# Both token norms turned by DMAs, feed-forward maxima one step later, ScalarE applying the second norm

## The reference, cut to what matters

```
x = x + _L0_conv_ref(_gn(x), ...)                      # gate, two experts of four, ReLU between w1 and w2
t = _to_tokens(x)                                      # (32, 784, 96)
t = t + _L1_attn_ref(_ln_t(t), qkv_w, ..., proj_b)     # 12 heads of 8, A = sum over tokens of fk * fv, out = q A
t = t + _L1_ffn_ref(_ln_t(t), W1, b1, W2, b2)
# _ln_t:  (v - mean) / sqrt(var + 1e-5) over the 96 channels of a token
# _L1_ffn_ref: y = x @ sign(W1).T + b1; y is scaled by 128 / max|y| of its group and clipped; gelu;
#              the same with W2.  There are 5 groups of 6 images; images 30 and 31 give zero.
x = _from_tokens(t, x)
```

## Time and profile before

| | us |
|---|---|
| median of 3 runs (lowest to highest) | 776.96 (775.61 to 778.39) |
| the profiled execution's own time | 777.66 |
| its span in the trace | 776.0 |
| PE busy | 727.5 (94%) |
| DVE busy | 679.7 (88%) |
| ACT busy | 473.3 (61%) |
| POOL busy | 221.5 (29%) |

### The profile page before, as it was taken

How to read it: one execution, slowest core, us unless ns; L and a number is a source line. 1 busy time by engine, 2 the same in 40 slices (tenths; PEclk the granted TensorE clock), 3 DMA queues, 4 the chain that set the end, 5 groups by cost and what they waited for, 6 DMA issues and landing times.

```text
span 776.0 us, 15540 instructions
## 1 busy us (share of the span) xinstructions
PE 727.5 (94%) x4858; PEld 480.5 (62%) x4858; DVE 679.7 (88%) x2058; ACT 473.3 (61%) x669; POOL 221.5 (29%) x301
## 2 busy tenths in 40 slices
PE   6798899999999999999999999999999899999991
PEld 3465466666766666766666766666766566555550
DVE  3577589999999999999999999999999678999997
ACT  2455356665555665555665555665554699999980
POOL 2352223324333324333324333324332001111110
PEclk8889899999999999999999999999999999999996
DMA  9970111111111111111111111111110101564446
GB/s 216 199 186 1 32 33 32 34 47 31 31 47 31 31 47 31 31 47 31 31 47 31 31 47 31 31 47 31 31 31 16 31 1 19 91 127 60 62 63 140
DMA packets 17663, 41.40 MB, mean 53 GB/s; under 512 B 4553, under 2 KB 4839, under 8 KB 17639
## 3 DMA queue, kind: packets, MB, share of 16 engines
q1 hardware_dynamic: 14552, 33.27, 16.4%
q0 software_dynamic: 2688, 7.23, 6.6%
q10 hardware_dynamic: 399, 0.60, 0.3%
HBM read 22.28 MB, written 18.67 MB: 53 GB/s over the span
## 4 chain that ended last, share of the span: by engine, by line
PE 63%; DVE 18%; issue 6%; ACT 5%; SPq 3%; DMA 2%; POOL 2%; DVEq 1%; ACTq 0%; POOLq 0%
PE slot L1071 15%; PE slot L1055 13%; PE slot L1284 6%; PE slot L1077 5%; PE slot L917 5%; PE slot L1082 5%; PE slot L1131 5%; DVE stage L1659 4%; PE slot L1118 4%; ACT stage L799 4%; SPq L476 3%; DVE stage L1646 3%; DVE y2max L1765 2%; DVE xn L1788 1%; PE slot L1342 1%
## 5 line engine op out<-in xcount | busy, mean ns | idle before, releaser
L1071 PE MATMUL slot<-hT,w2s 128*96 128x392 f32 x372 | 132.6, 492 | 0.8 <-DVE w2s L1532 0.8
L1613 DVE TENSOR_SCALAR tok<-tok,ln_mv,ln_rs 112x96 f32<-112x96 f32 x434 | 109.0, 322 | 2.0 <-POOL ln_rs L624 1.9
L624 POOL TENSOR_TENSOR ln_rs<-ln_ve,pow_half 112x7 f32<-112x7 f32 (+2 forms) x92 | 105.1, 1142 | 7.2
L799 ACT ACTIVATE stage<-slot,kv_bias,kv_unit 112x768 f32<-112x768 f32 (+1 forms) x62 | 53.1, 907 | 86.6 <-PE slot L1118 86.6
L621 POOL TENSOR_TENSOR ln_ve<-ln_mv,ln_eps 112x7 f32<-112x7 f32 (+2 forms) x92 | 18.3, 199 | 296.1 <-DVE ln_mv L1595 296.1
L792 ACT ACTIVATE hT<-slot,b1c,w_unit 128x784 f32<-128x784 f32 x93 | 93.1, 1004 | 15.8 <-PE slot L1055 13.2
L1082 PE MATMUL slot<-big,W1b 96*128 (+1 forms) x360 | 89.3, 329 | 0.0
L1071 PEld LDWEIGHTS slot<-hT,w2s 128*96 128x96 f32 x372 | 58.6, 163 | 45.0 <-issue 42.9
L1619 DVE TENSOR_REDUCE ymax<-slot 128x784 f32 (+1 forms) x90 | 84.5, 966 | 0.0
L1077 PE MATMUL slot<-big,W1b 99*128 (+1 forms) x360 | 84.4, 329 | 0.0
L854 ACT ACTIVATE hT<-slot,s 128x784 f32<-128x784 f32 x90 | 80.2, 914 | 6.1 <-DVE stage L1646 3.2
(11 more groups left out here) (252 smaller groups left out, 1455.4 us busy)
## 6 DMA issues: line engine op xcount, KB each, us to landing
xs<-in_x SPq DMA_DIRECT2D x32, 294.0 KB, 2.9
out<-h_second SPq DMA_DIRECT2D x32, 294.0 KB, 2.6
big<-in_x SPq DMA_DIRECT2D x7, 1176.0 KB, 15.5
out<-h_second POOLq DMA_DIRECT2D x24, 294.0 KB, 4.2
big<-out SPq DMA_DIRECT2D x1, 1764.0 KB, 10.5
out<-big SPq DMA_DIRECT2D x6, 294.0 KB, 2.7
big<-in_x SPq DMA_DIRECT2D x2, 588.0 KB, 24.5
con<-shape_consts ACTq DMA_DIRECT2D x1, 445.5 KB, 6.3
```

What stands on the lines that cost most here:

```text
L624: nc.gpsimd.tensor_tensor(ln_rs[n][:, j0:j1], ln_ve[n][:, j0:j1], pow_half[0:TOK, j0:j1], ALU.pow).then_inc(ln_rstd[part], 1)
L799: nc.scalar.activation(ekv[:, j0:j0 + n, :], chunks(k, n, 256, 2 * C), ACT.Exp, bias=kv_bias[:, :], scale=kv_unit[0:TOK, 0:1]).then_inc(e_ ...
L1071: ins = mm(S[k][0:C, h, 0:HALF], w2s[:, v, t, :], src[:, t, h * HALF:(h + 1) * HALF], start=t == 0, stop=t == last, skip_group_check=True)
L1613: ins = V.tensor_scalar(src[:, j, :], src[:, j, :], ln_mv[n][:, j, 0:1], ln_rs[n][:, j:j + 1], ALU.subtract, ALU.mult)
```

## The change

Neither norm's tokens are transposed on PE any more. ACT makes a float16 high part of the tokens as they stand (112 tokens on the partitions, seven chunks padded from 96 to 128 columns), DVE the low part, and SP turns each part with one transposing DMA, from SBUF to SBUF: x1 into `xh1_hi` and `xh1_lo`, x2 straight into `big`. The padding carries the rows of ones (one for the attention's bias, three for the feed-forward bias), which is what L668 and a memset did before. The pads are written by POOL once, after the setup tensors whose memory they reuse.

The second norm is applied by ACT as scale and shift (seven activations, `apply2`), for which POOL forms -mean and its product with 1/sqrt; its moments are taken in one part. The maxima of the feed-forward tiles are taken for image i-3 instead of i-2: the first tile stands on PE behind mix and ahead of keys and values, in slot 2, and waits for both parts of x2; the second (tile 2, slot 0) stands behind A, the third (tile 1, slot 2) behind St's product. The hidden tiles run in the order 1, 0, 2, and mix in the same; t2's transposes stand between the first and the second mix. Image 29's three tiles come after the loop, ahead of the last keys and values, and the filling matmuls there are gone. On POOL, `xn_rest` goes first in a step and waits no longer for the norms. On SP, a step has four transposing DMAs beside the load and the store, in a written order.

```diff
+            def move_x1(i):
+                sp.wait_ge(x1_hi_ready, i)
+                if isinstance(i, int) and i == 1:
+                    sp.wait_ge(pads_ready, 1)
+                else:
+                    sp.wait_ge(ao_ready, i - 1)
+                sp.dma_start_transpose(turned(xh1_hi[:, 0:HW]),
+                                       x1_hi[:, :, :].rearrange("p j c -> p (j c)")).then_inc(x1_hi_moved, 16)
+                sp.wait_ge(x1_lo_ready, i)
+                sp.dma_start_transpose(turned(xh1_lo[:, 0:HW]),
+                                       x1_lo[:, :, :].rearrange("p j c -> p (j c)")).then_inc(x1_lo_moved, 16)
...
+            for i in range(LAST):
+                if i >= 1:
+                    move_x1(i)
+                if i >= 3:
+                    move_x2_low(i - 3)
+                if i >= 2:
+                    store_last((i - 1) // 2, (i - 1) % 2)
+                if i < LAST - 2:
+                    load_next(i // 2, i % 2)
+                if i >= 2:
+                    move_x2_high(i - 2)
+            move_x2_low(QIMAGES - 1)
+            store_last(LAST // 2 - 1, 1)
+            move_x1(LAST)
             store_last(LAST // 2, 0)
...
+            def x1_high(i):
+                act.wait_ge(xh1_ready, i)
+                nc.scalar.copy(x1_hi[:, :, 0:C], tok1[:, :, :]).then_inc(x1_hi_ready, 1)
+            def apply2(f):
+                act.wait_ge(ln_shift, f + 1)
+                for j in range(CHUNKS):
+                    ins = nc.scalar.activation(tok2[:, j, :], tok2[:, j, :], ACT.Identity,
+                                               scale=ln_rs[1][:, j:j + 1], bias=ln_nm[:, j:j + 1])
+                ins.then_inc(xh2_ready, 1)
...
@@ TensorE, one step
+                    pe.wait_ge(h_ready, 3 * i + 1)
+                    mix(1, 1, 1, first=1)
+                    if norm2:
+                        pe.wait_ge(t2_ready, i - 1)
+                        to_tokens(3, t2T[r], tok2_in_psum)
+                    pe.wait_ge(h_ready, 3 * i + 2)
+                    mix(1, 1, 0, first=1)
+                    pe.wait_ge(h_ready, 3 * i + 3)
+                    mix(1, 1, 2, first=1).then_inc(y_mixed, 1)
+                if ffn:
+                    pe.wait_ge(x2_hi_moved, 16 * (i - 2))
+                    pe.wait_ge(x2_lo_moved, 16 * (i - 2))
+                    ffn_next(0)
                 if attend:
-                    pe.wait_ge(xh1_hi_ready, i)
+                    pe.wait_ge(x1_hi_moved, 16 * i)
...
@@ VectorE, one step
+                if attend:
+                    x1_low(i)
...
                 if ffn:
-                    dve.wait_ge(tok2_ready, f + 1)
-                    stats2(f)
+                    x2_low(f)
+                if norm2:
+                    dve.wait_ge(tok2_ready, i - 1)
+                    stats(1, tok2, i - 1)
...
+                if ffn:
+                    absmax(f, 0)
...
                 if ffn:
-                    for t in range(SPLIT):
-                        absmax(f, t, t)
+                    absmax(f, 1)
+                    absmax(f, 2)
...
+                if experts:
+                    apply1(i)
```

More of the change, by code:

```diff
@@ L616, in _ @@
             nc.gpsimd.tensor_scalar(kv_bias[:, :], kv_bias[:, :], -1.0, 1.0, ALU.add, ALU.mult).then_inc(kvw_ready, 1)
[L618 to L625, removed]
+            pool.wait_ge(kvw_ready, 2)
@@ L632, in step @@
[L632 to L636 removed]
+                    shift(i - 2)
                 rstd(0, i)
@@ L835, in step @@
                     nc.scalar.copy(R_hi[:, :], S[3][0:C + 1, 0, 0:C]).then_inc(r_hi_ready, 1)
-                if experts and next_:
+                if next_:
                     norm_image(m + 1, r, i + 2)
-            step(0, 0, attend=False, ffn=False, between=True)
+                if norm2:
+                    x2_high(i - 2)
+            step(0, 0, attend=False, norm2=False, high=False, between=True)
             for i in range(1, FIRST):
-                step(i // 2, i % 2, ffn=i >= 2)
+                step(i // 2, i % 2, norm2=i >= 2)
                 if i == 2:
@@ L847, in _ @@
             step(LAST // 2 - 1, 0, next_=False)
-            step(LAST // 2 - 1, 1, next_=False)
+            step(LAST // 2 - 1, 1, next_=False, high=False)
             def gelu_tile(g, b, t, k=None):
@@ L1219, in step @@
                     mix(1, 1, 0, h_second)
-                elif experts and not first:
-                    pe.wait_ge(h_ready, 3 * i + 2)
-                    mix(1, 1, 0)
-                if attend and not second:
-                    x1_to_channels()
-                if second:
                     mix(1, 1, 2, h_second)
@@ L1589, in chunk_stats, with stats @@
                 return ins
-            def moments(part, count):
-                n, j0, j1 = LN_PARTS[part]
-                wait_apart(dve, ln_stats[part], count, dve_passed)
-                for j in range(j0, j1):
+            def stats(n, src, count):
+                chunk_stats(src, range(CHUNKS)).then_inc(ln_stats[n], 1)
+                wait_apart(dve, ln_stats[n], count, dve_passed)
+                for j in range(CHUNKS):
                     ins = V.bn_aggr(ln_mv[n][:, j, :], ln_st[:, j, :])
-                ins.then_inc(ln_mean[part], 1)
@@ L1617, in absmax, with apply1, x1_low @@
-            def absmax(f, t, k):
-                dve.wait_ge(y_ready, 3 * f + t + 1)
+                ins.then_inc(ln_mean[n], 1)
+            def apply1(i):
+                dve.wait_ge(ln_rstd[0], i + 1)
+                for j in range(CHUNKS):
+                    ins = V.tensor_scalar(tok1[:, j, :], tok1[:, j, :], ln_mv[0][:, j, 0:1], ln_rs[0][:, j:j + 1],
+                                          ALU.subtract, ALU.mult)
+                ins.then_inc(xh1_ready, 1)
+            def x1_low(i):
+                dve.wait_ge(x1_hi_ready, i)
+                V.tensor_tensor(x1_lo[:, :, 0:C], tok1[:, :, :], x1_hi[:, :, 0:C],
+                                ALU.subtract).then_inc(x1_lo_ready, 1)
@@ L1734, in step @@
                                            ALU.mult, ALU.add).then_inc(t2_ready, 1)
-                if ffn and not last:
-                    absmax(f, SPLIT, SPLIT)
-                if experts and not last:
-                    apply(0, tok1, i).then_inc(xh1_ready, 1)
             for i in range(FIRST):
-                step(i // 2, i % 2, attend=i >= 1, ffn=i >= 2)
+                step(i // 2, i % 2, attend=i >= 1, norm2=i >= 2, ffn=i >= 3)
                 if i == 1:
```

340 lines of the change are left out of this document (165 added, 175 removed).

## The result

| | before | after |
|---|---|---|
| median, us (lowest to highest) | 777.56 (775.61 to 778.39), 4 runs | 855.65 (849.41 to 859.06), 4 runs |
| profiled execution, time / span | 777.7 / 776.0 | 853.6 / 851.9 |

The changed kernel is slower: the ratio is 1.100, 95% interval 1.093 to 1.107. The direction was forecast; the size was not: 802 was predicted, and 856 lies outside the range of 763 to 850.

A forecast was written before the change was run, and what follows sets the result against it. TensorE, issuing in order almost without a hole, was taken to bound the kernel, VectorE nearly as full. 777.7 us + 23 (29 steps at 17.45) + 2 (ends) = 802.7, or 802 as a median; range 763 to 850.

The forecast's parts named there:

- ACT's activations: Seven second-norm activations on ACT: 1.7 us a step, up to 2.3, hidden below PE's step; St's lateness beyond set to nothing.
- PE's saving: PE's step without the normed tokens' transposes: 16.15 us if no transfer is late, at most 0.5 us saved.
- DVE's times and the queue's start: Subtractions on DVE 0.80 us each, x2_low made by T+5.5; SP issues x1 high at T+3.9.
- T: Start of the step's first hidden matmul on PE, from which the forecast counts times in us.
- Landing: Transfer of x2's low part: 3.2 us from issue to landing, so there at T+8.9.
- L: Issue-to-landing time of a transposing DMA: bounds 2.0 to 4.2 us, taken as 3.2.
- Issue time: SP's time to issue each transposing DMA in its queue, taken as 0.9 us.
- r: Issue time of one transposing DMA on SP: bounds 0.34 to 1.4 us, taken as 0.9.
- The rival of a bound by SP's issue: SP's queue: r of 1.4, x2 low at T+10.4, step 18.9 us, kernel 846 us; chance 0.20.
- The clock in the loop: Half clock behind a PE hole, a hidden pair 0.86 us for 0.5: only some 3 us at the ends, for the range.
- The ends: Outside the steady steps: step 2 takes 2.0 us less, the part behind the loop +4; net +2 us.
- a landing like the plain store's: No-change rival, x2 low's transfer: L 2.55 to 2.65 us, step 16.65, kernel 778 us; chance 0.08.

The follow-up runs named there:

- e11_older_split: e1_older with ScalarE rearranged: next norm moved ahead of its image's cast, second norm's activations split four before St, three behind R_hi; 766.06 us.
- e1_older: Changed kernel with feed-forward tiles reading token parts one image step older, all transfers still made; 782.50 us, ratio 1.0086.
- e6_low_split: Changed kernel with x2's low part made and sent at the end of the step before, and ScalarE rearranged as in e11_older_split; 770.53 us.
- e7_order_split: e5_order with the rearranged ScalarE of e6_low_split; 785.86 us, ratio 1.0108.
- e2_fill: Changed kernel with eight filling matmuls of 512 columns ahead of TensorE's wait for x2's parts; 840.15 us, ratio 1.0807.
- e8_four_chunks: Changed kernel with x1's two transfers turning only four of seven chunks from image 2 on; 845.30 us, ratio 1.0873.
- e10_one_chunk: Changed kernel with x1's two transfers turning only one of seven chunks from image 2 on; 839.53 us, one run.
- e5_order: Changed kernel with x2's low part ahead of x1's low part on VectorE and in SP's queue; 803.82 us, ratio 1.0322.
- e3_apply_late: Changed kernel with ScalarE's seven second-norm activations moved behind its copy of R_hi; 894.79 us, ratio 1.1518.

## Why the prediction was wrong, step by step

The runs split the 2.45 us by which a steady step grew (19.08 less 16.63). The rows add up by construction, since each is the difference of two runs:

| part | us a step | from |
|---|---|---|
| what the edit saves when nothing is late | -0.64 | e11_older_split 15.99, before 16.63 |
| ACT's activations, St late | +0.47 | e1_older 16.46 less 15.99 |
| wait for x2's low part | +2.04 | 18.50 less 16.46 |
| clock behind that wait | +0.58 | 19.08 less 18.50 |

What speaks for each row beyond the sum: ACT's other order gave 0.47, 0.45 and 0.47 on three different kernels (e11_older_split, e6_low_split, e7_order_split); the wait is 2.02 from start to start in the trace; and e2_fill takes the clock's part away while the wait stays. The first row includes ACT's other order, in which the next norm also stands elsewhere, so it is the saving of the edit in its best form and not of the edit as it was made.

- **PE's saving.** Forecast 16.15 at best, measured 15.99. Right, to 0.16.
- **DVE's times and the queue's start.** Forecast x1 high at T+3.9 and x2_low made by T+5.5; measured 406.42 - 402.56 = T+3.86, and 0.85 after 407.20, T+5.49. Right to a tenth, subtractions included (0.77 from start to start, for 0.80).
- **Landing.** L taken as 3.2, measured 3.09 in this place. Right.
- **Issue time: the first step that failed.** r was taken as 0.9, by the 138 KB SBUF-to-SBUF row; it is 1.21 to 1.29. Together with the gaps between issues, x2 low was issued at T+6.45, not T+5.7, and landed at T+9.54, not T+8.9; PE was ready for it at T+7.52, not T+7.66. The wait, in the forecast's own terms, is 2.0 instead of 1.3: +0.7. The upper bound of 1.4, by a small parameter load, would have been nearer. The rival of a bound by SP's issue gave 846, for r = 1.4; the queue is what holds x2 low back, as it says, though e8_four_chunks and e10_one_chunk refute its reason by the tile. On the Trainium skill, DMA: Bandwidth & Descriptors, Why a DMA increments its semaphore by 16 and not by 1: its count per tile led me to an estimate of four times the ordinary issue, which 1.21 beside 0.34, 3.6 times, nearly bears out, but the trace does not agree with the count itself, since 7 tiles cost 1.12. The factor of four was loose besides: 49 times 32 is 1568 cycles, three times the 512, and four only if the 512 come on top. Advanced Engine Details and Errata, X-Bar Transpose (TRN2), as fast as ordinary: the landing of 2.7 to 2.8 beside the store's 2.8 comes near, though for two thirds of its bytes; the issue does not agree.
- **The clock in the loop: the second.** I had the earlier trace rows, a 2.65 us hole with a pair at 0.86 behind it, and kept it for the ends only, 3 us in the range. The forecast itself put a hole of 1.3 us in each of 29 steps and priced them at full clock. With the 1.9 that came it costs 0.58 a step, 17 us. At e5_order's 0.54 it costs nothing; no run has a hole of 1.3, so whether the forecast's own hole would have been free stays open.
- **ACT's activations: the third.** 1.7 in all, up to 2.3, were forecast from a copy of 97 columns (0.24 each); they take 2.61 (373 ns from start to start; the 457 ns of the groups' row count each by itself, with the overlap). The text had named the point: over 2.3, St comes late, "a term that I set to nothing". It was 0.47: in e1_older the product with St starts 0.40 later than in e11_older_split, and what follows it another 0.07.
- **The ends.** +2 forecast (step 2 included); measured +2.7, the 75.9 less the 73.2 by which the 29 steps from image 3's first hidden tile (115.52 for 119.11 before) to the loop's last matmul grew. The sum is right, its parts are not, and that is luck. What follows the loop grew by 6.3 instead of 4, though keys and values begin 8.7 behind its last matmul, for 8.4 forecast. Step 2, forecast 2.0 shorter, took 18.5 for 18.0. And image 2 started 4.1 earlier, which the forecast did not have: image 0's transposes start at 77.12 for 81.46 already, and why is open (in the edits image 2 starts anywhere from 96.6 to 99.8). The idle time behind the loop was forecast as about 4 us and is 4.48, with six matmul pairs at half clock behind it.
- **Readings that were off and changed nothing.** The clock's slices in the earlier trace rows are at 9 from the sixth to the last but one, not from the fourth: the fifth is an 8. For a landing like the plain store's, 5.5 + 2.6 is T+8.1, which makes a step of 16.6 and not 16.65.

In the forecast's terms a step should have been 17.45 and was 19.08: -0.16 for the saving, +0.74 for the wait, +0.58 for the clock, +0.47 for ACT, together 1.63, 47 us over 29 steps. The profiled execution took 853.6, 51 more than the 802.7. The other 4 are the loop's first steps, which were longer than the steady ones (19.15 is the mean with them), the ends, and rounding.

## What to carry to other kernels

Take a transfer that replaces engine work by its place in the queue: count every issue ahead of it at its own price, and ask where its consumer stands; here the same four transposes hold PE up by 2 us a step or not at all, 70 us in all, by the position of one subtraction and one issue. Price each new hole of an otherwise full TensorE twice, once for itself and once for half clock that can follow it, from a hole of similar length in the trace, and as a chance: here about half of equal holes cost it. A mean busy share of 61% is no slack: look for the chain that the inserted work stands in (ACT from R_hi to the ReLUs), and pair a move into it with a move out of it.

## What the runs showed of the hardware

- A transposing DMA from SBUF to SBUF holds the issuing engine 1.21 us (high parts) to 1.29 (low parts) for 196 KB, and 1.12 to 1.23 for a seventh of it; an ordinary store behind it 0.57 instead of 0.34.
- From issue to landing such a transfer took 2.7 us (median, x1's high part, 196 KB), 2.3 with four chunks of seven and 2.2 with one; as the third in a row 3.09.
- The kernel's DMA packets rose from 14552 to 115736 on that queue, and the engines' instructions were not measurably slower for it: in e1_older, 200 to 500 us, the mean of ACT's copy of 112x672 is 718 ns for 717 before, of DVE's maximum 972 for 966, of POOL's `xn_rest` 1668 for 1682.
- Falls of TensorE's clock, in one profiled execution of each kernel and among the steps between 150 and 600 us: behind holes of 2.42 us in 10 steps of 21 (e3_apply_late), of 1.86 in 13 of 23, of 1.79 in 8 of 23, of 1.70 in 6 of 23 (e10_one_chunk), of 0.54 in none. The length of one hole does not decide it: neighbouring steps with equal holes differ, and in the changed kernel the hole of 2.91 that ends at 77.12 has full clock behind it (77.74: 0.49 a pair, granted clock 0.99), while at 97.00 the clock is at 0.50 and PE's timeline of the 19 us ahead names no wait over 0.8 us.
- Seven activations on 112x96 float32 in SBUF with scale and bias per partition took 2.61 us where DVE's seven applications of a norm to the same tiles took 1.76.
